# Relative attention: two kinds of products write PSUM with a step of 16 elements, and ScalarE copies the banks in (head, query) order

## The reference, cut to what matters

```python
qk   = jnp.einsum('bhqd,bhkd->bhqk', qh, kh)
r_k  = _rel_emb(rk_table, Sq, Sk)                 # one row for each (query, key) distance
q_rk = jnp.einsum('bhqd,qkd->bhqk', qh, r_k)      # "placing"
attn = jax.nn.softmax((qk + q_rk) / scale, axis=-1)
w1   = jnp.einsum('bhqk,bhkd->bhqd', attn, vh)    # "first weighting"
r_v  = _rel_emb(rv_table, Sq, Sk)
w2   = jnp.einsum('bhqk,qkd->bhqd', attn, r_v)    # "second weighting"
out  = (w1 + w2).transpose(0, 2, 1, 3).reshape(B, Sq, E)
```

## Time and profile before

| | |
|---|---|
| median of three executions | 2883.41 us |
| the profiled execution, its own time | 2882.69 us |
| its span, first to last instruction | 2880.9 us |
| TensorE busy | 2106.3 us (73%) |
| VectorE busy | 1270.5 us (44%) |
| ScalarE busy | 941.3 us (33%) |
| mean granted clock of TensorE | 0.788 |

### The profile page before, as it was taken

How to read it: one execution, slowest core, us unless ns; L and a number is a source line. 1 busy time by engine, 2 the same in 40 slices (tenths; PEclk the granted TensorE clock), 3 DMA queues, 4 the chain that set the end, 5 groups by cost and what they waited for, 6 DMA issues and landing times. The chain is left out here.

```text
span 2880.9 us, 62464 instructions
## 1 busy us (share of the span) xinstructions
PE 2106.3 (73%) x25348; PEld 1633.1 (57%) x25348; DVE 1270.5 (44%) x2402; ACT 941.3 (33%) x1484; POOL 559.0 (19%) x523
## 2 busy tenths in 40 slices
PE   4777777773774597979888888887956776766764
PEld 3454445543663476767676767676744554444542
DVE  3444444435773254545454545454525762111112
ACT  2333333331221244434343434343314442111110
POOL 1111111100001010101010101010010004888881
PEclk8888989976887577878787878787776777898895
DMA  4445455421223212222222222222011214656556
GB/s 96 82 85 92 90 95 95 85 59 57 67 68 123 49 49 44 60 47 58 42 60 46 57 50 56 50 53 53 13 24 59 69 66 109 123 120 127 132 115 186
DMA packets 255381, 216.84 MB, mean 75 GB/s; under 512 B 70100, under 2 KB 234430, under 8 KB 255024
## 3 DMA queue, kind: packets, MB, share of 16 engines
q1 hardware_dynamic: 221008, 178.48, 26.8%
q0 software_dynamic: 24576, 27.05, 5.6%
q10 hardware_dynamic: 9568, 7.87, 0.9%
HBM read 147.08 MB, written 72.45 MB: 76 GB/s over the span
## 5 line engine op out<-in xcount | busy, mean ns | idle before, releaser
L1394 PE MATMUL r_ps_s<-r_q,r_rk 96*128 96x32 bf16 x4096 | 268.1, 235 | 83.0 <-DMA r_q<-parts_scratch 66.5
L1270 ACT ACTIVATE r_score<-r_ps_s 128x512 f32<-128x512 f32 x256 | 257.9, 1042 | 183.7 <-PE r_ps_s L1394 182.4
L1394 PEld LDWEIGHTS r_ps_s<-r_q,r_rk 96*128 96x128 bf16 x4096 | 251.0, 123 | 106.9 <-issue 83.4
L1165 DVE TENSOR_TENSOR r_score<-r_score,r_ps_t 128x1024 f32<-128x1024 f32 x128 | 155.4, 1217 | 208.5 <-PE r_ps_t L1405 208.4
L1186 DVE TENSOR_TENSOR r_score<-r_ps_s,r_score 128x512 f32<-128x512 f32 x256 | 162.9, 683 | 100.4 <-PE r_ps_s L1425 98.9
L1471 PE MATMUL r_ps_b<-r_score,r_rv 128*32 128x32 f32 x8192 | 181.5, 261 | 13.9 <-issue 13.5
L1471 PEld LDWEIGHTS r_ps_b<-r_score,r_rv 128*32 128x32 f32 x8192 | 153.7, 134 | 39.3 <-issue 39.1
L1947 DVE TENSOR_TENSOR e_hT<-e_sil,e_ps_gu 128x256 f32<-128x256 f32 x64 | 26.9, 421 | 324.2 <-ACT e_sil L1969 319.0
L1976 ACT ACTIVATE e_y<-e_ps_y,e_rows 128x256 f32<-128x256 f32 x128 | 53.6, 470 | 324.9 <-DMA slots_in_scratch<-e_y,k_token 166.1
L313 DVE TENSOR_REDUCE a_row_max<-a_ps_s 128x2 f32<-128x512 f32 (+1 forms) x192 | 127.5, 685 | 64.4 <-PE a_ps_s L478 58.0
L1425 PE MATMUL r_ps_s<-r_q,r_k 96*128 96x128 bf16 x1024 | 102.5, 239 | 71.3 <-DMA r_k<-parts_scratch 46.3
(11 more groups left out here) (293 smaller groups left out, 4413.5 us busy)
## 6 DMA issues: line engine op xcount, KB each, us to landing
a_q<-parts_scratch SPq DMA_DIRECT2D x96, 128.0 KB, 4.4
a_k<-parts_scratch SPq DMA_DIRECT2D x96, 128.0 KB, 4.2
r_q<-parts_scratch SPq DMA_DIRECT2D x48, 256.0 KB, 4.1
r_k<-parts_scratch SPq DMA_DIRECT2D x48, 256.0 KB, 4.3
e_wg<-in_L_ffn_expert_wg SPq DMA_DIRECT2D x64, 128.0 KB, 2.4
e_wu<-in_L_ffn_expert_wu SPq DMA_DIRECT2D x64, 128.0 KB, 3.0
e_wd<-in_L_ffn_expert_wd SPq DMA_DIRECT2D x64, 128.0 KB, 3.3
rows_w_scratch<-m_row SPq DMA_DIRECT2D x8, 640.0 KB, 3.2
```

The costliest lines, as they stand in the source:

```text
L1165: dve.tensor_tensor(part, part, bcast(ps_t[m % 2][:], NT), ALU.add).then_inc(shifted, 1)
L1270: act.activation(score[1 - t][:, c // 8, :, q0:q0 + 16].rearrange("p h q -> p q h"), ps_s[c % 2][:].rearrange("p (q h) -> p q h", h=BH), A ...
L1394: ins = pe.matmul(ps_s[c % 2][:, n * BH:(n + 1) * BH], rk6[:, j:j + P], q6[:, :, q], start=True, stop=True)
```

## The change

In both kinds of products the output's access pattern changes from 32 adjacent float32 columns to 32 columns with a step of 16, starting at the query's place. The bank then lies in (head, query) order, with 16 queries adjacent for each head. The two ScalarE copies read the bank from its first to its last column as before, and write `score` and `w2_raw` in runs of 16 adjacent elements. Operand sizes, counts of instructions, their order, the waits and the DMAs are as before.

```diff
-                        act.activation(score[1 - t][:, c // 8, :, q0:q0 + 16].rearrange("p h q -> p q h"),
-                                       ps_s[c % 2][:].rearrange("p (q h) -> p q h", h=BH), ACT.Copy).then_inc(place_copied, 1)
+                        act.activation(score[1 - t][:, c // 8, :, q0:q0 + 16],
+                                       ps_s[c % 2][:].rearrange("p (h q) -> p h q", h=BH), ACT.Copy).then_inc(place_copied, 1)
...
-                        act.activation(w2_raw[:, :, 16 * n:16 * n + 16].rearrange("p h q -> p q h"),
-                                       ps_b[n][:].rearrange("p (q h) -> p q h", h=BH), ACT.Copy).then_inc(w2_copied, 1)
+                        act.activation(w2_raw[:, :, 16 * n:16 * n + 16],
+                                       ps_b[n][:].rearrange("p (h q) -> p h q", h=BH), ACT.Copy).then_inc(w2_copied, 1)
...
-                            ins = pe.matmul(ps_s[c % 2][:, n * BH:(n + 1) * BH], rk6[:, j:j + P], q6[:, :, q],
+                            ins = pe.matmul(ps_s[c % 2][:].rearrange("p (h q) -> p q h", h=BH)[:, n, :], rk6[:, j:j + P], q6[:, :, q],
...
-                                    ins = pe.matmul(ps_b[n // 16][32 * j:32 * j + 32, (n % 16) * BH:(n % 16 + 1) * BH],
+                                    ins = pe.matmul(ps_b[n // 16][32 * j:32 * j + 32, :].rearrange("p (h q) -> p q h", h=BH)[:, n % 16, :],
```

## The result

The changed kernel takes 2855.45 us (2848.64 to 2860.55), beside 2880.92 us (2873.46 to 2888.25) for the kernel before, a ratio of 0.9912 [0.9896, 0.9929]. It is faster by 0.9%, 25 us, where 2880 and no measurable change were forecast. The profiled executions have spans of 2853.6 and 2880.9 us, 27.3 apart.

A forecast was written before the change was run, and what follows sets the result against it. TensorE was taken to set the pace, with ScalarE near it. From 2882.7 us, 1.4 for the query cast and 1.3 at the block's end, 2.7 together, and 0 for the products gave 2880; own range 2868 to 2890, whole range 2866 to 2955.

The forecast's parts named there:

- The products: Placing and second weighting: stepped output columns change TensorE's time by 0; a gain excluded, at most 28 ns more per 32 columns.
- The copies: Both ScalarE copies fall to 600 ns, 127 us less of ScalarE, but only 2.7 us less in the kernel (bounds 4.5 and 0).
- the one at the block's end: Second weighting's copies lead to the tail's transposes; TensorE waits on that three times, 0.45 us saved each, 1.3 us together.
- The other: End of t = 0 placings: the next round's query cast starts 0.2 us sooner in seven rounds, 1.4 us together.
- The room in the period: Stepped columns fit between product starts: 58 ns within 60.6 in placing, 57 within 81 in second weighting, so no delay.
- the guess of two accesses: In both products, a stepped column read as two PSUM accesses where there was one; still fits the periods, forecast sum unchanged.
- The upper price: Most a stepped product column could add, taken from ScalarE's stepped copy: 0.87 ns each, 28 ns for 32 columns.
- First rival: Stepped output slows second weighting alone, 28 ns a set of four products, 32 us, total 2915; chance 0.13.
- Second rival: Stepped output adds time in placing too, 101 us for both, total 2984, or 2952 with placing alone; chance 0.11.
- The third rival: The copies do hold TensorE, 36.3 us before the scores and 2.9 before placing, total 2844; chance 0.10.
- The fourth: Rival: the copy stays at 1042 ns, since runs of 16 are not a whole bank; nothing moves, 2883; chance 0.05.
- ScalarE's idle time before L1270: Sign that the forecast is right: ScalarE's wait before the placing copy, 182.4 us, grows by about 100 us.

## Why the prediction was wrong

**The step that failed is "The products. … From below: nothing is taken away from a product, … so a gain is excluded."** It bounded what a product costs, and let the product's time stand for the stage's time. The products' starts came out as written, but the stage is 33 us shorter over the kernel, because in a placing with doubled columns TensorE's clock comes back about 6 us earlier in most rounds and does not fall again before the placing ends. The products, which go at 58 ns at either clock, hid this; the projections and the spreading of maxima between them go in about half the time (0.97 us for 1.83, 0.59 for 1.05). With the 10 us given back in the scores this is the -23.1 us. I had the row for it: the placing of a t = 0 step at a granted clock of 0.68 in the earlier trace rows, beside 1.00 in its last 1.9 us. I read "TensorE busy 37.00 of 37.00" there, concluded that only TensorE's own work counts, and took the clock as given. A stage that TensorE bounds at 0.68 could gain from the clock alone; so a gain from the products was open, and the lower end of the range, 2866, was too high. (It lies 2 us below the 2868 that the text derives, for which it gives no reason.)

**The copies**: right within their bounds. 597 ns each against 600; -2.7 us with bounds of -4.5 and 0 against -3.7 [-6.9, -0.6]. Of the two parts of the sum, the one at the block's end came out: its three waits are 0.30, 0.59 and 0.41 us shorter in the changed kernel, 1.3 together. The other was mis-sized: the cast of the queries starts 0.07 us sooner before the scores, not 0.2. That they are covered by TensorE's work was right too: with 1044 ns and stepped products the kernel had the full gain.

**The room in the period**: right in result, and two cycles a column fit the guess of two accesses. The upper price of 0.87 ns more a column was near what a step costs at 1.2 GHz where it shows, 0.83 ns ((213 - 107) / 128), and twice that at 2.4 GHz, 0.41 ((109 - 56) / 128). It shows in the scores, not in placing, where by the estimate 53 ns fit into 58, nor in second weighting. *First rival* (second weighting alone slower): false, 64 products in 1.31 us against 1.30, and 0.9981 with that half alone. *Second rival*: false, 1.94 us as before.

**The third rival** (copies hold TensorE): false by the short copies alone. It had the right sign for the wrong mechanism, and the 36.3 us of the earlier trace rows were, as argued, the keys' DMA: the wait for it is 5.52 us after [5.92 in rows 4], with copies that end 0.45 us sooner. **The fourth**: false.

**Two smaller readings.** ScalarE's idle time before L1270 grew from 183.7 to 252.4 us, by 69 and not 100: the 33 us that the placings lost were idle time of ScalarE, and 105 - 33 is 72. And the last sentence before the forecast, that a gain of tens of us would mean waits for a bank hidden in TensorE's full windows, was false as well: the windows were full of work, much of it at half clock (0.68 on average in the earlier trace rows).

**What stays open.** That unpaired output columns change the granted clock rests on eleven kernels sorted by this one property (late in the placing, half clock in 30 of 30 rounds against 0 of 36), on pairs against a step of 2 above all. That it acts through the second cycle of a column is argued from the scores, not shown in placing. What the chip measures to grant the clock was not seen, nor why ten rounds of 36 rose late.

## What to carry to other kernels

A window in which an engine is busy from end to end need not be at its floor while its granted clock is below 1.00, as the placing here shows: read the clock beside the busy time, and bound a change of TensorE's work on both sides where the clock may move. Where something else set the period of products, columns alone in their 8 bytes of PSUM cost nothing and even helped; where columns set it, they took double the time, and pairs are what to try there. And a permutation was free on the reading side of PSUM where it cost ScalarE 445 ns a bank on the writing side of SBUF.

## What the runs showed of the hardware

- A float32 column alone in its 8 bytes of PSUM takes two TensorE cycles: 128 columns in 109 ns instead of 56 at 2.4 GHz, in 213 instead of 107 at 1.2 GHz (128 columns with a step of 4). Adjacent pairs with a step of 32 between them behave as adjacent columns in placing, in duration (235 ns) and clock.
- With the same instructions starting at the same times for 14.5 us, the clock rose 14.5 us into a placing with doubled columns and 21.3 us into one with adjacent columns; over rounds 1 to 6 it rose after 13.8 to 15.1 us in 26 of 36 placings with doubled columns, and after 19.9 to 22.1 in all 30 with adjacent columns or pairs. Half clock returned late in all 30 of these placings, and in none of the 36.
- Reading PSUM with a step is free for ScalarE (597 ns with a step of 32 and without; 1044 with a step of 16 and 1042 without, where the write is stepped in both) and VectorE (686 ns with a step of 4, 684 without). A copy to SBUF costs 597 ns in runs of 16, 607 in runs of 2 and 1042 with every element 512 bytes from the last.
